# A feed-forward net with its second layer one step behind the first, and four slots for gathered rows

## The reference

```python
x = x + gnn(layernorm(x), edges) + mix(layernorm(x))
xn = layernorm(x)
weights = xn @ wr + br
_, idx = top_k(weights, 6250)
sel_idx = idx[:6249]
sel = xn[sel_idx]
h = gelu(sel @ w1 + b1)            # 256 -> 1024
y = (h @ w2 + b2) * weights[sel_idx]
out = x + xn, with y added in the rows sel_idx
```

## Time and profile before

| | us |
|---|---|
| median of 3 runs | 3189.77 (3181.39 to 3196.99) |
| the profiled execution's own time | 3184.44 |
| its span in the trace | 3182.7 |
| PE busy (share of the span) | 2431.4 (76%) |
| DVE busy | 1325.7 (42%) |
| ACT busy | 960.6 (30%) |
| POOL busy | 1617.3 (51%) |
| first to last matmul of both layers of the feed-forward net | 2873.1 to 3169.9 |
| mean granted clock, of 1 | 0.85 |

### The profile page before, as it was taken

How to read it: one execution, slowest core, us unless ns; L and a number is a source line. 1 busy time by engine, 2 the same in 40 slices (tenths; PEclk the granted TensorE clock), 3 DMA queues, 4 the chain that set the end, 5 groups by cost and what they waited for, 6 DMA issues and landing times.

```text
span 3182.7 us, 50782 instructions
## 1 busy us (share of the span) xinstructions
PE 2431.4 (76%) x13646; PEld 1983.4 (62%) x13647; DVE 1325.7 (42%) x3288; ACT 960.6 (30%) x2185; POOL 1617.3 (51%) x1719
## 2 busy tenths in 40 slices
PE   1487887876777787777777777777787789939998
PEld 0366666765555565655655655665666677729998
DVE  8433333332332333333333333333343368884444
ACT  8322222321121111211111111111111159924544
POOL 2566666665666666666666556565655400003332
PEclk6689999997888788878888888878887899959999
DMA  9644454543334333333333333333333249812221
GB/s 304 186 148 147 148 155 143 154 142 121 113 112 122 115 114 112 111 115 116 112 110 114 111 108 114 107 115 109 109 110 109 87 165 309 304 66 64 68 67 45
DMA packets 229948, 412.28 MB, mean 130 GB/s; under 512 B 38194, under 2 KB 129716, under 8 KB 229887
## 3 DMA queue, kind: packets, MB, share of 16 engines
q0 software_dynamic: 81296, 224.22, 24.4%
q1 hardware_dynamic: 147774, 186.59, 17.4%
q10 hardware_dynamic: 816, 0.79, 0.1%
HBM read 315.13 MB, written 96.32 MB: 129 GB/s over the span
## 4 chain that ended last, share of the span: by engine, by line
PE 40%; another core or an unknown queue 21%; DVE 15%; issue 14%; DVEq 5%; ACT 4%; DMA 0%; POOL 0%; ACTq 0%; POOLq 0%; SPq 0%
PE ps L1435 9%; PE ps L1569 9%; PE ps L1358 4%; PE ps L1360 4%; PE ps L1477 3%; DVEq L421 3%; PE ps L1458 2%; PE ps L1403 2%; DVE onehot L777 2%; PE ps L1445 2%; DVE stats L847 2%; DVEq L777 1%; DVE work L959 1%; DVE onehot L956 1%
## 5 line engine op out<-in xcount | busy, mean ns | idle before, releaser
L631 POOL DMA_INDIRECT gath_raw<-xtab,srcI x1563 | 1477.7, 945 | 948.2 <-issue 447.4
L1358 PE MATMUL ps<-gath_raw,onehot 128*128 128x256 f16 x1956 | 525.1, 300 | 287.2 <-DVE onehot L777 199.7
L1360 PE MATMUL ps<-gath_raw,onehot 128*128 128x257 f16 x1956 | 527.5, 301 | 10.7 <-issue 10.6
L1435 PE MATMUL ps<-work,w_s 128*128 128x256 f32 x1568 | 441.4, 439 | 40.7 <-issue 39.7
L777 DVE SCALAR_TENSOR_TENSOR onehot<-ps,blkbase,dstF 128x512 f32 x489 | 352.9, 746 | 251.3 <-issue 221.9
L1358 PEld LDWEIGHTS ps<-gath_raw,onehot 128*128 x1956 | 211.5, 108 | 383.2 <-issue 343.0
L1435 PEld LDWEIGHTS ps<-work,w_s 128*128 128x128 f32 x1568 | 340.0, 223 | 104.4 <-issue 49.5
L787 DVE TENSOR_TENSOR agg<-agg,ps x98 | 41.5, 423 | 718.1 <-PE ps L1360 379.7
L1569 PE MATMUL ps<-split_raw 128*128 128x256 f32 x2376 | 292.6, 285 | 1.7 <-DVE split_raw L1069 1.5
L1569 PEld LDWEIGHTS ps<-split_raw 128*128 128x128 f32 x2376 | 287.8, 192 | 2.4 <-issue 1.9
L1403 PE MATMUL ps<-wkv_s,work 128*128 128x256 f32 x784 | 221.5, 445 | 70.1 <-ACT work L1175 65.7
(11 more groups left out here) (204 smaller groups left out, 3211.8 us busy)
## 6 DMA issues: line engine op xcount, KB each, us to landing
work<-x_in SPq DMA_DIRECT2D x98, 256.0 KB
ff_d<-work SPq DMA_DIRECT2D x49, 512.0 KB, 2.8
gath_raw<-xtab,srcI POOLq DMA_INDIRECT x1563
agg<-x_in SPq DMA_DIRECT2D x14, 896.0 KB, 7.3
xtab<-gath_raw SPq DMA_DIRECT2D x14, 896.0 KB, 4.9
xt_d<-work SPq DMA_DIRECT2D x49, 256.0 KB
q_d<-work SPq DMA_DIRECT2D x49, 256.0 KB
work<-q_d SPq DMA_DIRECT2D x49, 256.0 KB
```

The lines of the kernel that those rows point to most:

```text
L631: e.indirect_dma_start(out=gath[:, TPG * s + t, 0:2 * D], out_offset=None, in_=xtab[:, :], in_offset=bass.IndirectOffsetOnAxis(ap=srcI[:, ...
L1358: t.matmul(ps[:, ds(BG + k % 2, 1), 0:D], oh, gath[:, r, 0:D], start=False, stop=False, skip_group_check=True)
L1360: last = t.matmul(ps[:, ds(BG + k % 2, 1), 0:AGW], oh, gath[:, r, D:2 * D + 1], start=False, stop=q == TPG - 1, skip_group_check=True)
L1435: last = t.matmul(bank(BD + h)[:, o_ % 2, :], w1_s[:, c, o_ * P:(o_ + 1) * P], (mxT[s] if c < 2 else mynT)[:, c % 2, :], start=c == 0, sto ...
```

## The change

PE's body does the second layer of the step before, after the first layer of its own step and the next step's transposes. The first step has no second layer, and behind the loop stands the second layer of the last step. DVE's ending (weights, bias, output rows) moves likewise, into the new function f_end, called for the step before. The middle rows fh, fh_h and fh_l are held twice, and ACT waits for the second layer of two steps before in place of one. FSLOTS goes from 3 to 4, so gathered rows (frow), transposed halves (f_xh, f_xl) and output rows (fo) are held four times and the loops hold four steps a turn; frow and fo move into the buffer that earlier stages used for gathered edges. POOL's text changes only in the slot number of the scatter, which is still that of the step two before.

```diff
-FSLOTS = 3
+FSLOTS = 4
...
-        frow = [part(pool2, 2048 + 1024 * k, (2, 2 * D)) for k in range(FSLOTS)]
+        frow = [part(gath_raw, 1024 * k, (2, 2 * D)) for k in range(FSLOTS)]
...
-        fh = part(pool2, 8192, (HF // P, SB))
+        fh = [part(pool2, a, (HF // P, SB)) for a in (8192, 2048)]
...
                 if past(i, 2):
-                    scatter(i - 2, (s + 1) % FSLOTS, 2, P)
+                    scatter(i - 2, (s + FSLOTS - 2) % FSLOTS, 2, P)
...
+            def f_end(i, s, j, n):
...
             def f_body(i, s, j):
                 n = 1 if isinstance(i, int) and i == FSTEPS - 1 else 2
                 for h in range(4):
                     e.wait_ge(f_hh, 4 * i + h + 1)
...
                 if not (isinstance(i, int) and i == FSTEPS - 1):
                     f_low_x(i + 1, (s + 1) % FSLOTS)
-                e.wait_ge(f_in[s], 32 * j + 16 * n)
                 if past(i, 1):
-                    e.wait_ge(f_o, i)
+                    e.wait_ge(f_o, i - 1)
+                    f_end(i - 1, (s + FSLOTS - 1) % FSLOTS, j - 1 + (s + FSLOTS - 1) // FSLOTS, 2)
             steps(e, f_body, FSTEPS, FSLOTS, 2)
+            e.wait_ge(f_o, FSTEPS - 1)
+            f_end(FSTEPS - 1, (FSTEPS - 1) % FSLOTS, (FSTEPS - 1) // FSLOTS, 1)
...
                     e.wait_ge(f_h_ps, 4 * i + h + 1)
-                    if past(i, 1):
-                        e.wait_ge(f_y_ps, i)
+                    if past(i, 2):
+                        e.wait_ge(f_y_ps, i - 1)
...
+            def f_second(i, s, n):
+                if past(i, 1):
+                    e.wait_ge(f_yb, i)
+                for u in range(n):
+                    for c in range(HF // P):
+                        if u == 0 and c % 2 == 0:
+                            e.wait_ge(f_h, 4 * i + c // 2 + 1)
+                        last = split_products(bank(BF)[:, u, :], [h_[s][:, c, u * P:(u + 1) * P] for h_ in (fh_h, fh_l)],
+                                              [w[:, c, :] for w in (fw2_h, fw2_l)], c == 0, c == HF // P - 1)
+                last.then_inc(f_y_ps, 1)
...
                     f_T(i + 1, (s + 1) % FSLOTS, j + (s + 1) // FSLOTS, k)
                 if past(i, 1):
-                    e.wait_ge(f_yb, i)
...
+                    f_second(i - 1, (s + 1) % 2, 2)
             steps(e, f_body, FSTEPS, FSLOTS, 2)
+            f_second(FSTEPS - 1, (FSTEPS - 1) % 2, 1)
```

More of the change, by code:

```diff
@@ L399, in build @@
         fstg = [pool2[:, 1760 + 2 * k:1762 + 2 * k].bitcast(i32) for k in range(FSLOTS)]
-        frow = [part(pool2, 2048 + 1024 * k, (2, 2 * D)) for k in range(FSLOTS)]
-        f_xh = [part(pool2r, 5120 + 512 * k, (2, SB)) for k in range(FSLOTS)]
-        f_xl = [part(pool2r, 14848 + 512 * k, (2, SB)) for k in range(FSLOTS)]
-        fo = [part(pool2, 6656 + 512 * k, (2, D)) for k in range(FSLOTS)]
-        fh = part(pool2, 8192, (HF // P, SB))
+        frow = [part(gath_raw, 1024 * k, (2, 2 * D)) for k in range(FSLOTS)]
+        f_xh = [part(pool2r, 4096 + 512 * k, (2, SB)) for k in range(FSLOTS)]
+        f_xl = [part(pool2r, 6144 + 512 * k, (2, SB)) for k in range(FSLOTS)]
+        fo = [part(gath_raw, 1024 * FSLOTS + 512 * k, (2, D)) for k in range(FSLOTS)]
+        fh = [part(pool2, a, (HF // P, SB)) for a in (8192, 2048)]
         f_junk = part(pool2, 10240, (2, D))
@@ L408, in build @@
         fw2_s = part(pool2, 10752 + 2 * HF, (HF // P, D))
-        fh_h = part(pool2r, 16384, (HF // P, SB))
+        fh_h = [part(pool2r, a, (HF // P, SB)) for a in (16384, 18432)]
         fw1_h = part(pool2r, 20480, (2, HF))
         fw2_h = part(pool2r, 20480 + 2 * HF, (HF // P, D))
-        fh_l = part(pool2r, 8192, (HF // P, SB))
+        fh_l = [part(pool2r, a, (HF // P, SB)) for a in (8192, 2048)]
         fw1_l = part(pool2r, 10752, (2, HF))
@@ L1100, in f_body @@
                 last.then_inc(f_o, 1)
+            def f_body(i, s, j):
+                n = 1 if isinstance(i, int) and i == FSTEPS - 1 else 2
+                for h in range(4):
+                    e.wait_ge(f_hh, 4 * i + h + 1)
+                    c = slice(2 * h, 2 * h + 2)
+                    v.tensor_tensor(fh_l[s % 2][:, c, :], fh[s % 2][:, c, :], fh_h[s % 2][:, c, :].bitcast(f32),
+                                    ALU.subtract).then_inc(f_h, 1)
+                if not (isinstance(i, int) and i == FSTEPS - 1):
+                    f_low_x(i + 1, (s + 1) % FSLOTS)
+                if past(i, 1):
+                    e.wait_ge(f_o, i - 1)
+                    f_end(i - 1, (s + FSLOTS - 1) % FSLOTS, j - 1 + (s + FSLOTS - 1) // FSLOTS, 2)
             steps(e, f_body, FSTEPS, FSLOTS, 2)
+            e.wait_ge(f_o, FSTEPS - 1)
+            f_end(FSTEPS - 1, (FSTEPS - 1) % FSLOTS, (FSTEPS - 1) // FSLOTS, 1)
         @block.scalar
@@ L1291, in _, with f_high @@
             f_copy(0, 0)
-            def f_high(i, h):
+            def f_high(i, s, h):
                 e.wait_ge(f_g, 4 * i + h + 1)
-                a.activation(fh_h[:, 2 * h:2 * h + 2, :], fh[:, 2 * h:2 * h + 2, :], ACT.Copy).then_inc(f_hh, 1)
+                a.activation(fh_h[s % 2][:, 2 * h:2 * h + 2, :], fh[s % 2][:, 2 * h:2 * h + 2, :], ACT.Copy).then_inc(f_hh, 1)
             def f_body(i, s, j):
@@ L1299, in f_body @@
                     e.wait_ge(f_h_ps, 4 * i + h + 1)
-                    if past(i, 1):
-                        e.wait_ge(f_y_ps, i)
+                    if past(i, 2):
+                        e.wait_ge(f_y_ps, i - 1)
                     for c in (2 * h, 2 * h + 1):
-                        last = a.activation(fh[:, c, :], bank(BB + h)[:, c % 2, :], ACT.Gelu_apprx_tanh,
+                        last = a.activation(fh[s % 2][:, c, :], bank(BB + h)[:, c % 2, :], ACT.Gelu_apprx_tanh,
                                             bias=fb1_s[:, c:c + 1])
                     last.then_inc(f_g, 1)
-                    f_high(i, h)
+                    f_high(i, s, h)
                 if not (isinstance(i, int) and i == FSTEPS - 1):
```

## The result

The changed kernel takes 3372.77 us (median, 3359.72 to 3382.32); the kernel before takes 3189.7 beside it. The ratio is 1.0572, interval 1.0526 to 1.0618: slower by 183 us, where 165 were forecast.

A forecast was written before the change was run, and what follows sets the result against it. PE, busy at full clock, was taken to bound the feed-forward stage. After the change a circle of 17.5 us plus 1.9 for the clock, 19.4 a step against 11.94, adds 165 us to 3189.8: 3355 us, range 3300 to 3395.

The forecast's parts named there:

- T(0): PE's transposes of step 0 in the feed-forward stage; T(i) stands for those of step i.
- the wait of L1(1): Step 1's first layer on PE, with no second layer ahead, waits for its input: 2.8 us idle, once.
- the circle: Feed-forward stage: transposes, lagged second layer, ending, scatter, gather and next transposes wait in turn, 17.5 us a step at full clock.
- the 0.6 us that the lag wins at the end: Last step on PE: a wait goes away, about 14.29 us less 114 matmuls of 0.120 us, a gain of 0.6 us.
- Part 3: POOL's order: a gather stands behind the scatter's wait for the lagged layer, closing a loop of 17.5 us against 11.94.
- the wait for low halves: PE's second layer waiting for the low half of its last middle blocks, put at 0.07 us a step.
- part 1: PE's new order: gains of 1.6 and 0.6 us against 2.8 us idle once, +0.6 us in all.
- Part 4: PE's clock falls to 0.50 in each idle gap and rises about 4.0 us after restart, costing 1.9 us a step.
- A (clock holds): Rival: the loop of waits forms but PE's clock stays full, 42 us less than forecast, 3313 us; chance 6%.
- B (not slower): Rival: gathers still land within the first layer and PE stays the bound, 3190 us; chance 8%.
- C (the clock never lifts): Rival: the low clock lasts through the second layer, a step of 22.9 us, 3432 us in all; chance 3%.
- mean clock of 0.85: Sign of a right forecast: PE's granted clock in the feed-forward stage down to about 0.85 from 1.00.

The follow-up runs named there:

- run 1: Changed kernel with the scatter behind each gather being that of three steps before, not two; ratio 1.0016 to the kernel before.
- run 2: Kernel before with four slots and the moved buffers, but the second layer in its own step; ratio 0.9998 to the kernel before.
- runs 5 and 6: Changed kernel with the next transposes between the second layer's halves, ratio 1.0323; changed kernel with the row-number copy ahead of the scatter wait, ratio 1.0532.
- run 3: Changed kernel with 44 useless matmuls after each first layer from step 2 on; ratio 1.0490 to the kernel before, 17.77 us a step.

## Why the prediction was right, and what it mis-sized

Forecast 165 us more and measured 183, 3355 against 3373, inside the range. The account by the spans of the two first profiles (184.2 us), with the forecast beside it:

- Ahead of the stage: 4.8 us, forecast 0. The diff has nothing there, and medians of the kernel before itself lie between 3182 and 3190 on this chip.
- From T(0) to T(3): 4.6 us, forecast 2.5. T(1) to T(2) took 10.44 us for 8.9: the wait of L1(1), forecast at 2.8 us, comes as 2.5 us of idle, but the clock that this wait costs, 1.6 us in L1(1), was not forecast. T(2) to T(3) took 17.76 us where the circle was put at 17.5. The remaining 0.3 us lie between T(0) and T(1), where the kernels without the circle differ by 1.3 us among themselves (9.77 to 11.08).
- T(3) to T(24): 167.0 us, forecast 155. Here is the main error, 0.55 us in each of 21 steps.
- Behind T(24): 7.8 us, forecast 7.0. The 0.8 us wait of L2(24) for the shared bank was missed, and the 0.6 us that the lag wins at the end was counted.

**Part 3, the circle**, is shown: opening it (run 1) ends it, the slots alone (run 2) do not make it, and taking 24 matmuls or the copy out of it (runs 5 and 6) shortens it. Measured at full clock (run 3), by legs: to the bias 6.44 (6.32 worked out), to the output rows 1.74 (1.76), to the scatter 0.87 (0.86), scatters 2.29 (2.29), to the first gather 1.11 (1.14, with 0.1 of landing wait that is 0), between the gathers 1.72 (1.51), to the transposes 3.59 (3.6). The sum is 17.77 for 17.5. The leg that was off most, by 0.2 us, is the issue of the first gather, 1.43 us right behind the scatters where a row of before had 1.21. Of the 0.12 us in the first leg 0.07 is the wait for low halves that was deducted and does not exist (see part 1).

**Part 4, the clock**, had the mechanism right and the size low. From the transposes to the bias the changed kernel takes 8.67 us, 2.23 more than with the gap filled; forecast 1.9. I had taken the time to the rise of the clock from two gaps, 3.6 and 4.4 us, and within a step of the changed kernel it can be 5.2. The two gaps were behind different work and of a slightly different length, and the experiments show that this time moves with the gap. It also moves at a gap that stays the same: in the changed kernel, with gaps of 5.4 to 5.7 us, the time from the transposes to the bias runs from 7.7 to 9.1 us, a loss of 1.2 to 2.7. So a constant was the wrong form. What decides it from step to step was not settled.

The leg where the trace was preferred to the Trainium skill (DMA: Bandwidth & Descriptors, Anatomy of one DMA): the gathers of the changed kernel land after 3.3 to 4.6 us, 3.6 in the middle, by the trace's own statistic; the estimate of 2.6 us from the page's figure for 256 KB would have made the forecast worse by 20 us.

```profile
DMA to landing us min/median/max: 3.3/3.6/4.6
```

**Part 1** was wrong in one step that cost little: "So the waits that the change is to take off PE are worth 0.07 us a step." Run 1 takes every such wait off and keeps 11.95 us. The lag costs about 4 us and not 0.6: 1.6 us of gain did not exist, and 0.8 us of waiting for the bank and 1.6 us of low clock in L1(1) were not seen.

**Rivals.** A (clock holds) is excluded by run 3, which shows what it would have been. B (not slower) is what run 1 gives, 0.16% more than before; it needed one more step between a gather and the scatter ahead of it. C (the clock never lifts) is excluded by the windows of one step. The forecast of a mean clock of 0.85 for the stage met 0.84.

## What to carry to other kernels

When a stage is put one step behind, look at every queue whose text still counts in steps: an issue that waits for that stage's result now waits a step longer, and all that stands behind it in the same queue with it. Follow the waits once around; if the legs close to a circle, its length is the step, however idle each engine is. More buffers do not help where a buffer is not what is waited for, and the lag itself brings nothing where the engine is already busy without a break.

## What the runs showed of the hardware

Added work can shorten a step: 44 useless matmuls in a gap of 5.5 us kept TensorE's clock at 1.00 and took 2.2 us off each step of 20.0. The price of a gap in clock is not proportional to it: gaps of 2.8 to 3.0 us sometimes cost nothing and sometimes 1.1 to 2.7 us, gaps of 5.5 cost 1.2 to 2.7 and 2.2 in the mean, and gaps of 7.0 cost 1.3 in the mean. Behind a single wait of 2.5 us 1.6 were lost. The clock can fall after the engine has started again and not only in the gap, 1.4 us after it in the step shown. An indirect gather issued behind a copy and soon after scatters holds GpSimd for 1.43 us, right behind scatters without the copy for 0.99, and behind a copy without scatters ahead for 0.97; why the two together cost more was not tried. Chips gave the kernel before 2692 and 3185 us, with all of the difference ahead of the last stage; why was not tried.
